# A gated cross-attention and mixture-of-experts block: nine expert tiles are started before the last batches are routed

## The chip, the core and the metric

The kernel runs on one core of a Trainium2 chip. The metric is the device time of one execution in microseconds (us), lower is better. TensorE (PE) does the matrix products, with its weight loads (PEld) beside them; VectorE (DVE) and ScalarE (ACT) read what it leaves in PSUM; GpSimd (POOL) works on SBUF and issues the indirect DMAs; SyncE (SP) issues most of the other DMAs.

## The reference

Eight batches of 256 tokens with 512 features pass two residual blocks: a cross-attention over 256 context rows, then a layer of eight experts of which each token takes two.

```python
x = x + tanh(g_xattn) * xattn(layernorm(x), ctx, mask)      # softmax(q . ctx / sqrt(512)) @ ctx, one head
h = layernorm(x)
probs = softmax(h @ w_router.T); top_v, top_i = top_k(probs, 2); top_v /= sum(top_v)
g = einsum('th,eih->tei', h, w_gate); u = einsum('th,eih->tei', h, w_up)      # inner width 192
out = einsum('tei,ehi,te->th', silu(g) * u, w_down, comb)
x = x + tanh(g_ffn) * out
```

## The kernel before, in words

**Attention.** The 2048 tokens are 16 token tiles of 128 (two to a batch). A loop over steps `s` is written out for each engine, and in step `s` several tiles are in hand at once: on TensorE `t1(s)` transposes the normalised tile (line 914), `score(s - 1)` multiplies it with the context (930, 932), `tp(s - 2)` transposes the softmax (920), `pv(s - 2)` multiplies it with the context again (943), `t2(s - 3)` transposes the second normalisation (951) and `rt(s - 4)` multiplies that with the router (962). VectorE adds the attention to the tile of x (`x2`, line 652, which frees the PSUM bank `PO` for the next `pv`), takes its statistics (611) and sends them to GpSimd, which takes the root (`rstd`, 370). ScalarE normalises (`xln` 493, `x2ln` 501), takes the exponential (470), and moves PSUM to SBUF. ScalarE stores the sum to `out` and the normalised tile to `x2s` in HBM; SyncE stores the router's weights (`comb`) beside it.

**Expert weights.** The 40 units of the experts' weights (five for each expert) are loaded during attention. Each is split into a high part (`hi`, ScalarE, line 506) and a low part (`lo`, GpSimd, line 379). `SPLIT` says how many units belong to step `s`. Four units (`NU - NUA`) are left for the expert phase (`HOLD`).

**Routing.** For each batch VectorE picks two experts per token (`top2`, `ranks`), TensorE counts ranks (`cum`, 974 to 980), VectorE turns them into slot numbers (`slots`, 695 to 718: `TA`, `TB`), and TensorE adds them into a table (`tab`, 986). These pieces of VectorE (and `coefs`, the weights of the two experts) are the "side" work that `weave` puts between its attention work. When all eight batches are in the table, `tiles` finds which expert owns each tile of 128 slots (`sel`), and from table and `sel` come the rows of each tile (`IXG` to gather, `IXI` to add back), its expert number (`ER`) and expert column (`EJ`).

**Experts.** There are up to 39 tiles of 128 slots (here 36 run), sorted by expert. For tile `j` TensorE does `gu(j)` (twelve products with the gate and up weights, 1070 to 1074, into `S0` or `S1`), `tx(j + 1)` (four transposes of the gathered rows, 1060, into `A0` or `A1`), `down(j - 1)` (five products, 1093 to 1098, into `PO` or `PL`) and `th(j)` (two transposes of the hidden tile, 1083, into `PC` or `PTB`). ScalarE does `silu`, `xhi`, `yev` (564, the scaled result into one of five buffers `YT`) and `hhi`; VectorE does `mul` (872, 873), `xlo` (865), `coef` (885, 886) and `hlo` (878). GpSimd gathers tile `j + 6` (409) and adds tile `j` to `out` in HBM (435). Two experts may add to one row, so `fence` lets GpSimd wait, where a tile has another expert than the one before, until all earlier additions have landed.

## Time and profile before

| | us |
|---|---|
| median of three runs (lowest, highest) | 290.98 (290.82, 292.32) |
| the profiled execution: its own time | 291.58 |
| its span in the trace | 289.8 |
| TensorE busy | 255.7 |
| VectorE busy | 168.7 |
| GpSimd busy | 164.1 |
| ScalarE busy | 148.7 |

All rows come from the profiled execution. Matmuls are pipelined, so their durations overlap: what a tile costs TensorE is the distance between the starts of two tiles, not the sum of their durations.

### The profile page before, as it was taken

What the parts mean: (1) busy time and instruction counts of PE and PEld (TensorE: products, weight loads), DVE (VectorE), ACT (ScalarE), POOL (GpSimd) and SP (SyncE); (2) the same over time, 40 slices, a digit from 0 to 9 for tenths busy, and PEclk for the clock granted to TensorE, in tenths of its full rate; (3) what the DMA queues carried; (4) which work ended last, traced back from release to release, by engine and by line L of the source; (5) the groups of instructions that cost most, each with busy time, mean ns of one, the idle gap of its engine ahead of it and who ended that gap; (6) DMA issues with size and microseconds to landing.
All of it is one profiled execution on the core that took longest, in us unless ns stands there. A gap on an engine that the chain in (4) does not pass through costs nothing.

```text
span 289.8 us, 5422 instructions
## 1 busy us (share of the span) xinstructions
PE 255.7 (88%) x1501; PEld 217.7 (75%) x1501; DVE 168.7 (58%) x618; ACT 148.7 (51%) x310; POOL 164.1 (57%) x151
## 2 busy tenths in 40 slices
PE   0999998999999974477999999999999999999940
PEld 0877876677877653366899999999899999999920
DVE  4466778999977899950444444544444554444420
ACT  3469865687775644300455554554454455444430
POOL 1246557556564529225066686884765838748470
PEclk9999999999999997555999999999999999999995
DMA  6995999897998238007058576775894966868584
GB/s 220 385 380 168 344 349 285 329 296 272 302 313 299 99 97 280 1 14 206 5 83 146 104 131 127 138 137 98 157 171 100 165 141 108 174 95 167 121 127 57
DMA packets 25950, 52.08 MB, mean 180 GB/s; under 512 B 5248, under 2 KB 5376, under 8 KB 25920
## 3 DMA queue, kind: packets, MB, share of 16 engines
q0 software_dynamic: 8304, 19.83, 37.6%
...
## 4 chain that ended last, share of the span: by engine, by line
PE 62%; DVE 23%; issue 7%; ACT 3%; POOL 2%; DMA 1%; ACTq 0%; POOLq 0%; DVEq 0%
PE S L1070 9%; PE S L1071 9%; PE S L1074 9%; PE A L1060 6%; DVE st L611 4%; PE S L932 4%; PE PO L943 3%; DVE TB L718 3%; DVE X L652 3%; DVE TA L711 2%; PE PL L1093 2%; DVE dd L672 2%; PE A L914 1%; PE PO L1093 1%; PE PO L1095 1%
## 5 line engine op out<-in xcount | busy, mean ns | idle before, releaser
L435 POOL DMA_INDIRECT out<-YT,IXI x36 | 56.8, 1577 | 43.0 <-ACT YT L564 19.9
L1070 PE MATMUL S<-WGh,XTh 128*128 x144 | 52.4, 364 | 0.9 <-ACT XTh L543 0.9
L1071 PE MATMUL S<-WGl,XTh 128*128 x144 | 49.2, 342 | 0.0
L409 POOL DMA_INDIRECT XG<-x2s,IXG x39 | 38.5, 986 | 18.0 <-issue 9.1
L872 DVE TENSOR_TENSOR H<-SG,S 128x192 f32<-128x192 f32 x36 | 12.8, 354 | 48.3 <-ACT SG L550 40.7
L379 POOL TENSOR_TENSOR WGl<-WGl,WGh 128x512 fp32r<-128x512 f32 x24 | 30.5, 1275 | 14.5 <-ACT WGh L506 14.4
L550 ACT ACTIVATE SG<-S 128x192 f32<-128x192 f32 x36 | 11.9, 330 | 50.6 <-PE S L1074 49.1
L370 POOL TENSOR_TENSOR rs<-mv,CS 128x1 f32<-128x1 f32 x32 | 17.6, 551 | 30.8 <-DVE mv L617 30.8
L865 DVE TENSOR_TENSOR XTl<-A,XTh 128x512 fp32r<-128x512 f32 x37 | 25.6, 692 | 14.1 <-ACT XTh L543 13.1
L943 PE MATMUL PO<-CX,PT 128*128 128x512 f32 x64 | 31.2, 610 | 1.8 <-ACT PT L479 1.8
L1074 PE MATMUL S<-WGh,XTl 128*128 x144 | 31.5, 342 | 0.0
L932 PE MATMUL S<-CT,XLT 128*128 128x256 f32 x128 | 31.2, 388 | 0.0
L1070 PEld LDWEIGHTS S<-WGh,XTh 128*128 128x128 f32 x144 | 27.6, 192 | 1.7 <-issue 1.6
L1071 PEld LDWEIGHTS S<-WGl,XTh 128*128 128x128 f32 x144 | 27.8, 193 | 0.0
L543 ACT ACTIVATE XTh<-A 128x512 fp32r<-128x512 f32 x37 | 22.1, 598 | 9.5 <-issue 4.8
L932 PEld LDWEIGHTS S<-CT,XLT 128*128 128x128 f32 x128 | 23.9, 197 | 3.0
L1074 PEld LDWEIGHTS S<-WGh,XTl 128*128 128x128 f32 x144 | 26.1, 192 | 0.0
L611 DVE BATCH_NORM_STATS2 st<-X 128x6 f32<-128x512 f32 x32 | 22.0, 688 | 4.0 <-DMA X<-in_x 3.5
L1060 PE MATMUL A<-CS,XG 128*128 128x128 f32 x148 | 23.1, 281 | 1.1 <-DMA XG<-x2s,IXG 1.1
L501 ACT ACTIVATE Y<-X,nb,rs 128x512 f32<-128x512 f32 x16 | 13.0, 813 | 21.1 <-DVE nb L626 20.9
L1060 PEld LDWEIGHTS A<-CS,XG 128*128 128x128 f32 x148 | 19.0, 145 | 2.9 <-issue 1.4
L943 PEld LDWEIGHTS PO<-CX,PT 128*128 128x128 f32 x64 | 11.0, 191 | 10.0 <-issue 7.7
...
## 6 DMA issues: line engine op xcount, KB each, us to landing
...
```

What stands on the lines that cost most here:

```text
L379: pool.tensor_tensor(out=low, in0=raw[p], in1=hi[p].bitcast(fp32), op=ALU.subtract).then_inc(s_wl, 1)
L409: pool.indirect_dma_start(out=XG[:, j % NX, :], out_offset=None, in_=x2s, in_offset=bass.IndirectOffsetOnAxis(ap=IXG[:, j:j + 1], axis=0))\
L435: pool.indirect_dma_start(out=out, out_offset=bass.IndirectOffsetOnAxis(ap=IXI[:, j:j + 1], axis=0), in_=YT[:, j % NB, :], in_offset=None, ...
L543: act.activation(XTh[:, j % 2, :, :], (A0, A1)[j % 2][:, :].rearrange("p (k c) -> p k c", k=KC), ACT.Copy).then_inc(s_xh, 1)
L611: n = mark(dve.bn_stats(st[:, k % 2, :], src))
L865: dve.tensor_tensor(XTl[:, j % 2, :, :], (A0, A1)[j % 2][:, :].rearrange("p (k c) -> p k c", k=KC), XTh[:, j % 2, :, :].bitcast(fp32), ALU ...
L932: m = pe.matmul(SC[k % 2][:, 0:S], XLT[:, k % 2, c, :], CT[:, b % 2, c, :], start=False, stop=(c == KC - 1))
L943: m = pe.matmul(PO[:, :], PT[:, k % 2, c, :], CX[:, b % 2, c, :], start=(c == 0), stop=(c == 1))
L1060: m = pe.transpose((A0, A1)[j % 2][:, 128 * c:128 * c + 128], XG[:, j % NX, 128 * c:128 * c + 128], ident)
L1070: pe.matmul(o, XTh[:, j % 2, c, :], WGh[:, bass.ds(e, 1), c, :], start=(c == 0), stop=False)
L1071: pe.matmul(o, XTh[:, j % 2, c, :], WGl[:, bass.ds(e, 1), c, :], start=False, stop=False)
L1074: m = pe.matmul(o, XTl[:, j % 2, c, :], WGh[:, bass.ds(e, 1), c, :], start=False, stop=(c == KC - 1))
```

## The change

**The order.** A first list is made of the first four batches alone (`EB = 4`). Of the tiles that these batches fill wholly there are at least nine (`NE`), and nine are taken. Their numbers (`IXE`, `ERE`, `EJ[0:9]`) come from the table after batch 3, in step 16 (`whole`, `first_list`, `table`, `first_rows`, `first_experts`). The table is then started again for the last four batches and added to the first one (`Tsb`). The other tiles get the last list (`left`, `last_list`, `last_rows`, `last_tiles`), whose first tile of each expert stands behind those taken (`lql`). The expert loop starts right after the last `pv`. What was left of routing runs inside its first nine tiles: on TensorE between the four parts of a tile, on VectorE by the table `SIDES` (how many side pieces go after `mul`, after `coef`, after `hlo`), and on GpSimd by `GATHERS` (which gathers follow the addition of tile `j`). The number of tiles as a whole does not change.

**The memories.** `tx` uses `A0` alone, `down` uses `PO` alone, and `th` writes into the bank from which `mul` has just read, since `A1`, `PL`, `PC` and `PTB` are still in use by routing. `YT` has seven buffers instead of five. `XG`, the gathered rows, lies where attention's `X` was, so each of the first gathers waits until the tiles there are stored (`stored`).

**The weights.** All 40 units are split during attention, 12 more than before by the end of step 16 on GpSimd (`SPLIT`, `units`); from step 5 on (`LATE`) `hi` stands ahead of `x2ln` and `exp` on ScalarE. The 47 warming products on TensorE are gone.

**The fences.** Each addition `j` waits until `j - 2` has landed, and until `j - 1` has landed only where the expert changes and the ranges of rows of the two can meet.

```diff
-NB = 5
+NB = 7
-SPLIT = [0, 1, 1] + [2] * 15 + [1] * 4
-NUA = NU - 4
-HOLD = [3, 5, 7, 9]
+SPLIT = [0, 1, 2] + [3, 3, 2] * 4 + [3, 2]
+LATE = 5
+EB = 4
+NE = 4 * EB - 7
+NEP = (NE + 3) // 4 * 4
+NL = 32
+GATHERS = [[6, 7, 8], [], [], [9], [10, 11], [12, 13]] + [[j + 8] for j in range(6, NT - 8)] + [[]] * 8
+SIDES = [(2, 2, 5), (2, 2, 3), (1, 1, 2), (1, 1, 2), (2, 2, 2), (2, 2, 3), (1, 3, 4), (2, 1, 4)] + [(0, 0, 0)] * 31
...
@@ gpsimd
+            def landed(j):
+                pool.wait_ge(s_add[j % NB], 16 * (j // NB + 1))
+            def fence(j):
+                bits, i = (early, j - 1) if j < NE else (turns[(j - NE - 1) // 15], (j - NE - 1) % 15)
+                with pool.If((bits & (1 << i)) != 0):
+                    landed(j - 1)
...
+            pool.wait_ge(s_ixe, 1)
+            pool.wait_ge(s_sy[0], 16 * EB)
+            pool.wait_ge(s_sy[1], 16 * EB)
+            pool.wait_ge(s_scb[0], 16 * EB)
+            stored(9, 10)
+            gather(0)
+            rstd(mv2, 14, rs2, s_st2, s_rs2)
+            stored(11)
+            gather(1)
+            stored(12)
+            gather(2)
+            rstd(mv2, 15, rs2, s_st2, s_rs2)
+            odds(6)
+            stored(13)
+            gather(3)
...
             for j in range(NT):
                 with lives(pool, live, j):
+                    if j == 1:
+                        odds(7)
                     pool.wait_ge(s_y, j + 1)
-                    if j:
+                    if j >= 2:
+                        landed(j - 2)
+                    if j == NE:
+                        landed(j - 1)
+                    elif j:
                         fence(j)
...
+                    if j + NX == NE:
+                        pool.wait_ge(s_ixg, 1)
...
+                    for g in GATHERS[j]:
+                        gather(g)
@@ scalar
+            ev2(13)
+            store_y2(13)
+            evp(15)
+            xhi(0)
+            weigh(5)
+            act.activation(rsum[:, 0:1], rinv[:, 0:1], ACT.Silu)
+            store_x2(14)
+            x2ln(14)
@@ vector
+            side += [coefs(5), top2(6), taken()]
+            weave(queue(x2(14), first_xlo(), nbias(mv2, rs2, nb2, 14, s_rs2, s_nb2), x2(15)), 2)
+            side += [slots(5), ranks(6), coefs(6),
+                     braid(slots(6), queue(top2(7), braid(ranks(7), coefs(7)))),
+                     braid(slots(7), left()), last_tiles()]
...
+            def last_tiles():
+                dve.wait_ge(s_tab, B)
+                dve.tensor_tensor(Tsb[:, :], PTB[:, 0:128], Tsb[:, :], ALU.add).then_inc(s_tsb, 1)
+                yield
+                dve.wait_ge(s_ixp, 1)
+                dve.tensor_scalar(IXG[:, :], PC[:, 0:NL], float(T), float(T - 1), ALU.add, ALU.min).then_inc(s_ixg, 1)
...
@@ tensor
+            tp(14)
+            score(15)
+            first_list()
+            pv(14)
+            rt(12)
+            t2(13)
+            tp(15)
+            pv(15)
...
             tx(0)
+            rt(13)
...
+            pe.wait_ge(s_wl, NU)
             for j in range(NT):
                 with lives(pe, live, j):
                     gu(j, own[j])
+                    if j == 0:
+                        t2(14)
+                    if j == 1:
+                        t2(15)
+                        rt(14)
                     if j + 1 < NT:
                         tx(j + 1)
+                    if j == 0:
+                        cum(5)
+                    if j == 2:
+                        tab(5)
+                        cum(6)
+                    if j == 4:
+                        cum(7)
+                        count()
+                    if j == 5:
+                        tab(6)
+                    if j == 6:
+                        last_list()
+                        tab(7)
...
                     if j >= 1:
                         down(j - 1, own[j - 1])
+                    if j == 1:
+                        rt(15)
+                    if j == 6:
+                        last_rows()
                     th(j)
+                    if j == 0:
+                        tab(4)
```

The next rows are TensorE's order at the end of attention, from the last scores (`S<-CT,XLT`) to the transposes of the first gathered tile (`A<-CS,XG`). Before, 39 rows lie between the last `pv` (`PO<-CX,PT`) and that tile; here are the first of them.

```order
L932 MATMUL S<-CT,XLT 128x256 x4
L943 MATMUL PO<-CX,PT 128x512 x2
L962 MATMUL PL<-WR,Y2T 128x8 x4
L951 MATMUL A<-CS,Y 128x128 x4
L920 MATMUL S<-CS,P 128x128 x2
L943 MATMUL PO<-CX,PT 128x512 x2
L962 MATMUL PL<-WR,Y2T 128x8 x4
L951 MATMUL A<-CS,Y 128x128 x4
```

The same place in the change, up to the first product of expert tile 0:

```order
L1143 MATMUL S<-CT,XLT 128x256 x4
L1211 MATMUL A<-sel,Tsb 128x12
L1212 MATMUL A<-sel,CS 1x12
L1213 MATMUL A<-selE,CB 128x72
L1215 MATMUL A<-sel,Tsb 1x12
L1154 MATMUL PO<-CX,PT 128x512 x2
L1171 MATMUL PL<-WR,Y2T 128x8 x4
L1162 MATMUL A<-CS,Y 128x128 x4
L1131 MATMUL S<-CS,P 128x128 x2
L1154 MATMUL PO<-CX,PT 128x512 x2
L1295 MATMUL A<-CS,XG 128x128 x4
L1171 MATMUL PL<-WR,Y2T 128x8 x4
```

The first list (lines 1211 to 1215) stands between the last scores and `pv(14)`, and the first expert tile follows `pv(15)` at once.

The next rows are VectorE's order in step 16, from the row maximum of tile 15 (`nmx<-S`) to the sum of tile 14 (`X<-PO,rinv,X`). Before:

```order
L632 TENSOR_REDUCE nmx<-S 128x1
L661 MAX mx<-PL 128x8
L665 MAX_INDEX ix<-mx,PL 128x8 x2
L672 TENSOR_TENSOR dd<-mx 128x2
L644 RECIPROCAL rinv<-rsum 128x1
L695 TENSOR_TENSOR pr<-OH,PC 128x32
L700 TENSOR_REDUCE sl<-pr 128x4
L703 TENSOR_SCALAR Qi<-sl 128x4
L706 SCALAR_TENSOR_TENSOR rr<-Qi,sl 128x4
L652 SCALAR_TENSOR_TENSOR X<-PO,rinv,X 128x512
```

In the change, the later part of that stretch:

```order
L910 TENSOR_SCALAR IXE<-A 128x12
L790 TENSOR_SCALAR Qi<-sl 128x4
L793 SCALAR_TENSOR_TENSOR rr<-Qi,sl 128x4
L915 CAST ERE<-A 1x12
L798 TENSOR_TENSOR TA<-CS,Qi 128x512
L805 TENSOR_SCALAR TB<-CS,rr 128x128
L918 TENSOR_SCALAR EJ<-A,GB 128x72
L805 TENSOR_SCALAR TB<-CS,rr 128x128 x2
L922 SCALAR_TENSOR_TENSOR ME<-A,IXE 1x8
L805 TENSOR_SCALAR TB<-CS,rr 128x128
L764 TENSOR_TENSOR OH<-CS,ix 128x32
L925 TENSOR_REDUCE inc<-A 128x8
```

After these come `MS`, `Rt`, `rinv` and `Rn`, and then `X<-PO,rinv,X` of tile 14. The reading of the first list and the whole of `slots(4)` and `ranks(5)` now stand ahead of that sum.

The last piece is GpSimd's order at the end of attention. Before, six `lo` stand behind the root (`rs`) of tile 15, and six gathers in a row behind them:

```order
L370 TENSOR_TENSOR rs<-mv,CS 128x1
L379 TENSOR_TENSOR WGl<-WGl,WGh 128x512 x3
L379 TENSOR_TENSOR WD1l<-WD1l,WD1h 128x512
L379 TENSOR_TENSOR WD<-WS,WD 64x512 x2
L409 DMA XG<-x2s,IXG 128x520 x6
```

In the change:

```order
L407 TENSOR_TENSOR WD1l<-WD1l,WD1h 128x512
L424 DMA XG<-x2s,IXE 128x520
L398 TENSOR_TENSOR rs<-mv,CS 128x1
L424 DMA XG<-x2s,IXE 128x520 x2
L398 TENSOR_TENSOR rs<-mv,CS 128x1
L416 TENSOR_TENSOR e<-CS,dd 128x2
L424 DMA XG<-x2s,IXE 128x520
```

Gathers 1 and 2 now stand behind the root of tile 14, and gather 3 behind that of tile 15; no `lo` is left after the first gather.

## Rows read from the trace of the kernel before

**Rows 1.** Busy time of each engine, granted clock and DMA in four stretches

```profile
core 0: us, PE busy (x) PEld busy (x) DVE busy (x) ACT busy (x) POOL busy (x), PEclk, DMA share, GB/s
105.00:110.00 5.00, 4.02 (x47) 3.77 (x45) 4.30 (x20) 2.74 (x5) 2.71 (x4) 1.00 0.38 116
110.00:115.00 5.00, 2.53 (x12) 2.20 (x12) 4.90 (x10) 2.65 (x6) 4.86 (x5) 0.67 0.93 302
115.00:120.00 5.00, 1.30 (x11) 1.11 (x11) 4.83 (x28) 0.66 (x2) 1.19 (x1) 0.50 0.05 8
...
160.00:200.00 40.00, 40.00 (x236) 36.87 (x235) 18.75 (x61) 19.95 (x43) 28.04 (x22) 1.00 0.72 131
```

**Rows 2.** TensorE in order of time: start, us, what, idle before

```profile
103.23 1.98 PE L943 MATMUL PO<-CX,PT 128*128 128x512 f32 x4 [1.77 <-ACT PT L479]
105.05 0.95 PE L962 MATMUL PL<-WR,Y2T 128*128 128x8 f32 x8
...
106.96 0.64 PE L986 MATMUL PTB<-TB,TA 128*128 128x128 f32 x4
...
131.70 1.09 PE L1060 MATMUL A<-CS,XG 128*128 128x128 f32 x4 [1.15 <-DMA XG<-x2s,IXG]
133.56 0.68 PE L1070 MATMUL S<-WGh,XTh 128*128 x1 [0.77 <-ACT XTh L543]
...
139.40 0.44 PE L1070 MATMUL S<-WGh,XTh 128*128 x1 [0.15 <-ACT XTh L543]
...
272.80 0.42 PE L1070 MATMUL S<-WGh,XTh 128*128 x1
```

**Rows 3.** GpSimd's indirect DMAs in order of time

```profile
128.01 1.18 POOL L409 DMA_INDIRECT XG<-x2s,IXG  x1 [6.48 <-DVE IXG L847]
...
213.13 1.58 POOL L435 DMA_INDIRECT out<-YT,IXI  x1 [0.31 <-issue]
...
219.45 1.57 POOL L435 DMA_INDIRECT out<-YT,IXI  x1 [3.46 <-DVE cj L886]
...
281.56 1.55 POOL L435 DMA_INDIRECT out<-YT,IXI  x1 [1.18 <-ACT YT L564]
```

**Rows 4.** Two pairs of attention steps, from every second score on

```profile
60.15:72.18 12.03, 11.98 (x76) 9.22 (x74) 11.45 (x48) 8.77 (x20) 7.23 (x9) 1.00 0.86 287
...
84.31:95.82 11.51, 11.51 (x72) 8.74 (x71) 8.20 (x33) 8.40 (x18) 6.16 (x7) 1.00 0.76 256
```

**Rows 5.** Groups of instructions from 20 to 95 us

```profile
L379 POOL TENSOR_TENSOR WGl<-WGl,WGh 128x512 fp32r<-128x512 f32 x15 | 19.1, 1272 | 10.8 <-ACT WGh L506 10.8
...
L672 DVE TENSOR_TENSOR dd<-mx 128x2 f32<-128x2 f32 x5 | 4.4, 876 | 0.0
...
L681 DVE TENSOR_TENSOR MS<-OH 128x16 bf16<-128x16 f32 x5 | 4.2, 831 | 0.0
```

**Rows 6.** VectorE and GpSimd in order of time, a blocked and a free `MS`

```profile
67.52 1.27 POOL L379 TENSOR_TENSOR WGl<-WGl,WGh 128x512 fp32r<-128x512 f32 x1
67.54 1.28 DVE L681 TENSOR_TENSOR MS<-OH 128x16 bf16<-128x16 f32 x1
...
116.67 0.18 DVE L681 TENSOR_TENSOR MS<-OH 128x16 bf16<-128x16 f32 x1
```

**Rows 7.** VectorE and GpSimd around the sum of tile 14

```profile
101.49 0.74 DVE L652 SCALAR_TENSOR_TENSOR X<-PO,rinv,X 128x512 f32<-128x512 f32 x1
...
102.88 0.67 DVE L711 TENSOR_TENSOR TA<-CS,Qi 128x512 fp32r<-128x512 f32 x1
103.47 0.34 DVE L718 TENSOR_SCALAR TB<-CS,rr 128x128 fp32r<-128x128 f32 x1
...
104.53 0.61 POOL L370 TENSOR_TENSOR rs<-mv,CS 128x1 f32<-128x1 f32 x1 [2.98 <-DVE mv L617]
```

**Rows 8.** The move out of the bank of `down(j)`, and the start of `down(j + 1)`

```profile
147.30 0.69 ACT L564 ACTIVATE YT<-PL,cj 128x512 f32<-128x512 f32 x1 [0.56 <-PE PL L1098]
...
149.77 0.48 PE L1093 MATMUL PO<-WD1h,HTh 128*128 x1
```

698 lines of the change are left out of this document (426 added, 272 removed).

## The prediction

> **What bounds the kernel now.** I read the busy times by stretch first, since a page average mixes two stages, then the two long stages, then the piece between them.
>
> In the expert stage TensorE is busy without a gap at a granted clock of 1.00 [rows 1]. The first product of tile 1 starts at 139.40 and that of tile 35, the last, at 272.80 [rows 2]: 34 tiles in 133.4 us, 3.92 us each. From 272.80 to the end of the span are 17.0 us (the last `down`, the last addition at 281.56 [rows 3], its landing).
>
> In attention a pair of steps takes 12.03 us, of which TensorE is busy 11.98 and VectorE 11.45; the last pair, in which VectorE has only 8.20 us to do, takes 11.51 [rows 4]. So TensorE bounds this stage, with VectorE about half a microsecond a pair behind its back.
>
> Between the last `pv` at 103.23 and the first expert product at 133.56 [rows 2] lie 30.3 us. TensorE is busy 4.02, 2.53 and 1.30 us in the three stretches of 5 us from 105 on, while VectorE is busy 4.3 to 4.9 [rows 1]: the routing of the last batches goes round by VectorE. The granted clock drops to 0.50 there, so tile 0 takes 5.84 us to tile 1 (133.56 to 139.40), without a `down`. This piece is what the change attacks.
>
> **The change part by part.** I count from `pv(15)`, and call T0, T1, ... the starts of the products of tiles 0, 1, ...
>
> *VectorE ahead of the first tile.* In step 16 the sum of tile 14 (`X<-PO`) comes at 101.49 [rows 7], and `pv(15)` waits for the bank that it frees. The change puts ahead of it: `sel`, `selE`, `Tsb`, `IXE`, `ERE`, `EJ`, `ME` and `inc`, eight small operations, about 0.2 us each as an estimate from the free `MS` of 0.18 [rows 6], so 1.6; `TA` 0.67 and four `TB` of at most 0.34 [rows 7], so 1.9; and `OH`, `MS` and their like, 0.5. That is 4.0; I take 3.7, since a `lo` that blocked an operation here is gone. The sum comes at 105.2, `pv(15)` follows at 106.0 instead of 103.23 and ends 1.9 later. The first gather, made from `IXE` at about 101.5, is not late: before, gather 0 started at 128.01 and its rows were transposed from 131.70 on [rows 2, 3], 3.7 us, so it lands near 105.3. After `tx(0)` come `xhi` and the first product: at half clock this took 1.86 us (131.70 to 133.56), I take 1.4. T0 is 109.3.
>
> *Tile 0.* Gather 1 stands behind the root of tile 14 on GpSimd. Before, that root started 3.04 us after the sum of its tile (101.49 to 104.53 [rows 7]); now at about 107.8, the gather at 108.5, landed at 112.2. So `tx(1)` waits about half a microsecond, then `th(0)`, `tab(4)`, and `xhi(1)` behind `ev2(14)` on ScalarE: T1 is T0 + 5.0.
>
> *Extra work inside the tiles.* On TensorE, after T1: `rt` twice and `t2` once, 2.05 (`rt` 0.95 with its overlap [rows 2], so 0.8 each, and `tx`-like transposes 0.45); three `tab` of 0.5 to 0.64 [rows 2], two `cum` and the count, 2.2; the two lists, 0.9. Sum 5.2. Before, these lay in the piece that goes.
>
> *VectorE inside the tiles.* 52 side pieces go into tiles 0 to 7. VectorE is busy 18.75 of 40 us in this stage [rows 1], 1.84 per tile, so some 2 us a tile are free, and the pieces need as much (16 us over eight tiles by the durations above). Two of them wait: `Tsb` of the last list waits for `tab(7)`, and `IXG` for `last_rows` behind `down(5)`, and both stand ahead of `mul(6)`, so `th(6)` comes about 1.0 late. For the others I take another 1.0.
>
> *The late gathers.* Gather 9 can start when `IXG` is there, 5.9 us after T6; with 3.7 us it lands 9.6 after T6, while `tx(9)` comes in tile 8, about 12 after T6. Scatters 4 to 8 pile up behind it on GpSimd, which needs 1.58 us for an addition and 1.0 to 1.2 for a gather [rows 3], with a short gap after each some 3.2, against 3.92 of a tile, and seven `YT` buffers cover that. Nothing.
>
> *One bank instead of two.* `down(j + 1)` must wait until `yev(j)` has left `PO`. Before, that move ended at 147.99 and the next `down` started at 149.77 [rows 8]: 1.8 us to spare. `tx(j + 1)` waits for `xlo(j)`, which the last four products of `gu(j)` wait for anyway. Nothing.
>
> *Twelve more `lo` in attention.* Each takes 1.27 us on GpSimd [rows 5], 15.3 in all, which GpSimd has free (7.23 of 12.03 busy [rows 4]). But a `lo` holds up VectorE: `MS` started at 67.54, beside a `lo` from 67.52, and took 1.28 us where a free one takes 0.18 [rows 6]. On average `dd` took 876 ns and `MS` 831 [rows 5]. Over the stage these excesses (five `dd` and five `MS`, 0.7 each, and by estimate 1 us of others) come to some 8 us over 25 `lo` (15 of `WGl` [rows 5], ten of the other weights), 0.3 each. So twelve cost VectorE between 0 and 12 x 1.1 = 13 us; at 0.3 it is 3.8, and with what TensorE has to spare in a pair I take 3.0. The Trainium skill (SBUF — State Buffer, "SBUF: two separate sides") says that the pair of ports which VectorE and GpSimd share is locked for a whole instruction and the other engine waits. The trace agrees (1.28 beside 1.27 [rows 6]). By the rule alone, with each added `lo` meeting such an operation, the sum would be 286; by the average of the rows it is 276.
>
> *More loads in attention.* Weight units come earlier, eight in the place of six in three steps. The DMA share in a pair is 0.86 at 287 GB/s [rows 4], and weights are under a third of that by what each step loads, so a ninth more is still below full. Nothing, though a full queue would work like the upper bound above.
>
> **Sum.** T0 = 109.3 + 3.0 = 112.3. T35 = T0 + 5.0 + 133.4 + 5.2 + 1.0 + 1.0 = 257.9. The end is 17.0 later, 274.9, against 289.8: 14.9 us less. The profiled execution took 291.58 and the median is 290.98, so I take the difference from the median: 276.1.
>
> **The rivals.** *Better:* the pieces of VectorE fit and attention keeps its pace (its `lo` fill time in which ScalarE and VectorE wait). Then 3.0 + 2.0 + about 2 of the 2.8 at `pv(15)` come back: 269. Chance 0.15. For it: `hi` now stands in ScalarE's idle time ahead of `x2ln`. Against it: VectorE is busy 4.3 to 4.9 of 5 us around 105 to 120 [rows 1].
>
> *Attention stretches:* most of the 12 `lo` meet VectorE, 8 to 13 us instead of 3: 281 to 286. Chance 0.14. For it: VectorE is busy 95% in a pair.
>
> *The clock falls between the stages.* It stayed 1.00 with TensorE busy 4.02 of 5 us and fell in the next five [rows 1], where gaps of microseconds followed each other. In the change TensorE has gaps around `pv(15)` and `tx(1)`. At half clock tile 0 took 5.84 us, about 2.5 more than it would at the full one, so two such tiles give 279 to 281. Chance 0.09.
>
> *Slower than before:* the additions set the pace. Now each waits for the last but one, always. From 213.13 to the release of 219.45 a landing took 6.0 us [rows 3], so two in flight allow one per 3.0 us. If beside gathers and each other they took over 7.85 us (two tiles), half of the excess would be paid on each of 34 tiles; from 8.8 us on the kernel would be slower than before (0.45 x 34 = 15 us). At 9.2 us it takes 299. Chance 0.04. Against it: before, up to five were in flight and landed in 6.0.
>
> *It doesn't do what it says:* tile 0 waits for all weights (`s_wl`), for the first list and for stores of x. If one of these came 10 us late, the gain would shrink to 5: 286. Chance 0.04; GpSimd and the queues have room.
>
> **How the numbers follow.** The forecast, 271 to 280, holds 0.54. With the better case and the two middle ones the range is 268 to 286; outside lie parts of both ends. A change of 0.5% is about what a measurement of this kernel can tell from none. Faster 0.94, the same 0.02, slower 0.04.
>
> **What would show it.** In the profile after: a first `S<-WGh,XTh` near 112 at a clock of 1.00; the last one near 258; 3.92 us per tile from tile 9 on; pairs of attention steps of about 12.5 us instead of 12.03; `pv(15)` waiting for VectorE's sum. Wrong would be: waits of TensorE for a gather at tiles 3, 4, 5 or 9; `yev` waiting for an addition; a clock of 0.50 after 105.

## The result, and the profile after

The changed kernel takes 289.59 us (median of 16 runs, 286.96 to 291.94), the kernel before 291.19 (16 runs, 289.91 to 292.35). The ratio is 0.993, 95% interval [0.9903, 0.9957]: 0.7% faster, where 5% was forecast. The profiled execution of the change took 288.54 us, its span is 286.7 at a mean granted clock of 0.973. By the spans (289.8 and 286.7) the change gains 3.1 us, by the medians 1.6: the profiled execution of the change was 1.05 us under its median, that of before 0.4 over its own. I read the places below from the spans. Every place and every sum comes from one profiled execution, and executions of one kernel differ by up to 5 us (286.96 to 291.94), so a difference of about 1 us between two traces may be chance.

Busy time by stretch after: three pairs of attention steps (their bounds are starts of `score`), three stretches between the stages, and the long stretch of the expert stage that stands in [rows 1].

```profile
core 0: us, PE busy (x) PEld busy (x) DVE busy (x) ACT busy (x) POOL busy (x), PEclk, DMA share, GB/s
36.78:50.22 13.44, 11.75 (x71) 8.68 (x70) 11.35 (x40) 10.20 (x23) 9.85 (x11) 1.00 0.94 320
63.74:79.06 15.32, 12.38 (x75) 9.21 (x74) 15.15 (x52) 9.84 (x21) 9.00 (x10) 1.00 0.86 277
93.37:108.45 15.08, 11.83 (x72) 8.77 (x71) 12.96 (x44) 9.06 (x19) 7.43 (x8) 1.00 0.30 111
115.00:120.00 5.00, 3.07 (x8) 1.34 (x7) 2.84 (x12) 0.96 (x2) 0.00 (x0) 0.77 0.34 106
120.00:125.00 5.00, 4.77 (x25) 3.60 (x23) 2.73 (x17) 2.83 (x5) 1.60 (x2) 0.89 0.19 57
125.00:130.00 5.00, 3.11 (x23) 2.81 (x24) 4.14 (x23) 2.39 (x5) 3.22 (x4) 0.79 0.74 218
160.00:200.00 40.00, 39.87 (x234) 36.39 (x233) 19.69 (x73) 19.20 (x41) 23.73 (x20) 1.00 0.65 123
```

Before, the pair of [rows 4] took 12.03 us with TensorE busy 11.98 of them. Now a pair takes 15.32 with TensorE busy 12.38 and VectorE 15.15: in this pair VectorE has become the bound. In the other two neither engine is busy throughout (VectorE 11.35 of 13.44 and 12.96 of 15.08). The expert stage is as full as before. TensorE's own timeline shows the places (start, duration, line, operation):

```profile
108.45 1.89 PE L1143 MATMUL S<-CT,XLT 128*128 128x256 f32 x8
117.32 3.38 PE L1154 MATMUL PO<-CX,PT 128*128 128x512 f32 x4 [1.93 <-DVE X L739]
120.50 0.91 PE L1295 MATMUL A<-CS,XG 128*128 128x128 f32 x4
122.29 0.44 PE L1305 MATMUL S<-WGh,XTh 128*128 x1
127.55 0.78 PE L1295 MATMUL A<-CS,XG 128*128 128x128 f32 x4 [1.67 <-DMA XG<-x2s,IXE]
129.56 0.63 PE L1305 MATMUL S<-WGh,XTh 128*128 x1
269.91 0.42 PE L1305 MATMUL S<-WGh,XTh 128*128 x1
```

`score(15)`, the last scores, starts at 108.45; before it was 95.82, the end of the last pair of [rows 4]. From there to the first expert product (T0, 122.29) are 13.8 us, where before there were 37.7 (to 133.56 [rows 2]). So the change takes 23.9 us out between the stages and gives 12.6 back ahead of them. Tile 0 to the last tile (T35, 269.91) takes 147.6 against 139.2 before, since the rest of routing runs there: 8.4 back. From T35 to the end are 16.8. Together -23.9 + 12.6 + 8.4 - 0.2 = -3.1.

VectorE's small operations, 24 to 108 us, grouped by form (number, busy time, mean ns of one):

```profile
L774 DVE TENSOR_TENSOR Rt<-Rn,MS 128x8 bf16<-128x8 bf16 x5 | 4.7, 936 | 0.0
L798 DVE TENSOR_TENSOR TA<-CS,Qi 128x512 fp32r<-128x512 f32 x4 | 4.6, 1149 | 0.0
L713 DVE TENSOR_SCALAR nb<-mv,rs 128x1 f32<-128x1 f32 x22 | 4.6, 208 | 7.2 <-POOL rs L398 7.2
L817 DVE TENSOR_TENSOR cc<-cc,e 128x2 f32<-128x2 f32 x4 | 3.6, 909 | 0.1
L759 DVE TENSOR_TENSOR dd<-mx 128x2 f32<-128x2 f32 x5 | 2.9, 578 | 0.0
L768 DVE TENSOR_TENSOR MS<-OH 128x16 bf16<-128x16 f32 x5 | 1.8, 356 | 0.0
```

And two of them beside GpSimd, first VectorE's timeline, then GpSimd's:

```profile
66.78 1.01 DVE L759 TENSOR_TENSOR dd<-mx 128x2 f32<-128x2 f32 x1
68.42 0.16 DVE L790 TENSOR_SCALAR Qi<-sl 128x4 int32<-128x4 f32 x1
68.62 1.12 DVE L793 SCALAR_TENSOR_TENSOR rr<-Qi,sl 128x4 f32<-128x4 int32 x1
```

```profile
66.50 1.27 POOL L407 TENSOR_TENSOR WGl<-WGl,WGh 128x512 fp32r<-128x512 f32 x1
68.45 1.27 POOL L407 TENSOR_TENSOR WD1l<-WD1l,WD1h 128x512 fp32r<-128x512 f32 x1
```

`dd` ends at 67.79, just after the `lo` that ends at 67.77; `rr` at 69.74, just after the one that ends at 69.72. `Qi`, which started before the second `lo`, took 0.16. So far this is what the prediction said of `MS` and `dd` [rows 5, 6], but now other operations meet a `lo`: `Rt`, `cc`, `pc`, `Qi` and `TA`.

In the experiments I use three sums for each kernel, all from 24 us to `score(15)`. **Held** is the time by which the operations of VectorE's side work (`dd`, `MS`, `OH`, `Rt`, `Rn`, `pr`, `sl`, `Qi`, `rr`, `TA`, `TB`, `den`, `cc`, `pc`, `comb`) are longer than free ones: for each form its number times what its mean is above the mean of a free one (0.13 to 0.18 us for the small ones, 0.33 for `TB`, 0.68 for `TA`). `ntf`, `nti` and `rinv` are not among them (13 shows where that matters). **Root waits** is what `nb` waits for a root of GpSimd. **Chain** is how much of the chain of work that ended last (each step followed back from the kernel's end to what released it) runs through GpSimd's own work in that time, `lo` and roots. It names one path, and two paths can be nearly as long.

### The profile page after: what moved, and what is told of

Read it like the earlier page. It is cut to its first block, busy times and chain, and to the rows that moved or that the text cites. A ratio compares the mean times of both kernels' runs of the same rounds, so it can differ in the third digit from the quotient of the medians.

```text
span 286.7 us, 5375 instructions
## 1 busy us (share of the span) xinstructions
PE 250.5 (87%) x1464; PEld 210.7 (73%) x1464; DVE 176.5 (62%) x645; ACT 149.9 (52%) x308; POOL 165.7 (58%) x153
## 4 chain that ended last, share of the span: by engine, by line
PE 46%; DVE 21%; DMA 9%; issue 9%; POOL 8%; ACT 4%; ACTq 1%; POOLq 0%; DVEq 0%
PE S L1305 6%; PE S L1309 6%; PE S L1306 6%; DMA out<-YT,IXE 5%; PE A L1295 4%; DVE st L698 4%; PE PO L1154 3%; DVE X L739 3%; PE PO L1326 2%; PE PO L1331 2%; PE PO L1330 2%; PE PO L1327 2%; PE PO L1328 2%; DVE TB L805 2%; POOL WGl L407 2%
## 5 line engine op out<-in xcount | busy, mean ns | idle before, releaser
L492 POOL DMA_INDIRECT out<-YT,IXI x19 | 30.1, 1585 | 15.1 <-issue 5.7
L424 POOL DMA_INDIRECT XG<-x2s,IXG x30 | 29.5, 985 | 9.6 <-issue 5.5
L1154 PE MATMUL PO<-CX,PT 128*128 128x512 f32 x64 | 32.8, 637 | 2.5 <-DVE X L739 1.9
L582 ACT ACTIVATE XTh<-A 128x512 fp32r<-128x512 f32 x37 | 22.1, 599 | 11.3 <-PE A L1295 8.1
L603 ACT ACTIVATE YT<-PO,cj 128x512 f32<-128x512 f32 x26 | 17.9, 688 | 17.7 <-PE PO L1331 13.1
L1036 DVE TENSOR_TENSOR HTl<-S,HTh 128x256 fp32r<-128x256 f32 x36 | 15.3, 424 | 18.7 <-ACT HTh L595 16.2
L492 POOL DMA_INDIRECT out<-YT,IXE x7 | 11.2, 1594 | 19.1 <-DMA out<-YT,IXE 11.5
```

What stands on the lines that cost most here:

```text
L424: pool.indirect_dma_start(out=XG[:, xg(j), :], out_offset=None, in_=rows, in_offset=bass.IndirectOffsetOnAxis(ap=at, axis=0))\
L492: pool.indirect_dma_start(out=out, out_offset=bass.IndirectOffsetOnAxis(ap=to, axis=0), in_=yt(j), in_offset=None, compute_op=ALU.add)\
L582: act.activation(XTh[:, j % 2, :, :], A0[:, :].rearrange("p (k c) -> p k c", k=KC), ACT.Copy).then_inc(s_xh, 1)
L1154: m = pe.matmul(PO[:, :], PT[:, k % 2, c, :], CX[:, b % 2, c, :], start=(c == 0), stop=(c == 1))
```

## The experiments

The theory (A): the stretch of attention comes from `lo`, because a `lo` holds up a small operation of VectorE that meets it, and VectorE has no time to spare. Rivals: loads and stores that come earlier (DMA), ScalarE's new order, the units on GpSimd that make its roots late (B).

| kernel | us a unit on GpSimd | units begun before `score(15)` | held | root waits | chain | `score(15)` | T0 | span | time, us | ratio to before |
|---|---|---|---|---|---|---|---|---|---|---|
| before | 1.27 | 27 | 9.1 | 3.2 | 0.6 | 95.82 | 133.56 | 289.8 | 291.2 | |
| the change | 1.27 | 38 | 21.9 | 7.2 | 14.6 | 108.45 | 122.29 | 286.7 | 289.6 | 0.993 |
| 1 one fill | 0.53 | 38 | 0.8 | 3.8 | 0.6 | 93.57 | 104.31 | 269.2 | 272.65 | 0.936 |
| 2 twelve units fewer | 1.27 | 28 | 17.0 | 5.4 | 13.7 | 101.47 | 112.78 | 277.8 | 279.57 | 0.958 |
| 3 old place | 1.27 | 36 | 14.5 | 5.9 | 11.3 | 103.73 | 120.62 | 286.2 | 289.35 | 0.991 |
| 4 halves | 1.42 | 38 | 12.6 | 10.3 | 17.5 | 103.27 | 116.68 | 282.3 | 283.03 | 0.971 |
| 5 before, 40 units | 1.27 | 36 | 15.5 | 6.4 | 14.8 | 105.41 | 137.61 | 291.7 | 294.72 | 1.011 |
| 6 old place, last units early | 1.27 | 38 | 15.6 | 6.2 | 14.8 | 104.21 | 118.86 | 285.4 | 286.22 | 0.981 |
| 7 quarters | 1.70 | 37 | 7.5 | 15.8 | 38.3 | 105.69 | 121.46 | 286.5 | 288.22 | 0.987 |
| 8 old place and halves | 1.42 | 37 | 13.3 | 10.9 | 32.2 | 108.00 | 123.12 | 287.8 | 286.84 | 0.983 |
| 9 before, halves | 1.42 | 27 | 8.3 | 4.8 | 8.9 | 96.34 | 131.40 | 287.6 | 289.59 | 0.993 |
| 10 four fills | 0.66 | 38 | 0.5 | 4.9 | 0.0 | 93.99 | 104.64 | 269.3 | 271.37 | 0.932 |
| 11 a copy | 0.61 | 38 | 6.6 | 3.4 | 0.6 | 94.27 | 105.60 | 270.7 | 273.18 | 0.937 |
| 12 eight fills | 0.75 | 38 | 1.7 | 6.6 | 7.2 | 95.27 | 106.70 | 270.0 | 272.40 | 0.937 |
| 13 sixteen fills | 1.02 | 38 | 2.0 | 9.0 | 5.7 | 95.52 | 108.04 | 274.5 | 275.56 | 0.938 |

Each ratio is to runs of before taken beside it (medians 290.95 to 292.25). The four runs of 13 spread from 272.66 to 278.64; its ratio, taken without the highest, lies below that of the two medians (0.945).

**1. `lo` as a fill with zeros.** The low parts of the weights are zero; loads, high parts and every product stay.

```diff
-                pool.tensor_tensor(out=low, in0=raw[p], in1=hi[p].bitcast(fp32), op=ALU.subtract).then_inc(s_wl, 1)
+                pool.memset(low.bitcast(fp32), 0.0).then_inc(s_wl, 1)
```

> The changed kernel, but each of the 40 low parts is a GpSimd memset to zero in the place of the subtraction: same number, same order, same semaphores, same size written, nothing read (the low weights are zero, so the products with them add nothing). Theory 1 (the subtraction blocks VectorE's two-input operations, and that is what stretches attention): the excess of VectorE's small operations goes (cc, Rt, pc, TA at their free 0.16 to 0.68 us), the pairs of attention steps fall from 14 to 15 us to 12 or less, the last scores start at 92 to 96 instead of 108.5, and the whole takes 270 to 276. Rival A (GpSimd is only late with its roots because the low parts stand ahead of them): a memset is shorter too, so the stretch goes as well, but VectorE's small operations would have been as long as before. Rival B (twelve more high parts on ScalarE, their place ahead of x2ln, or the loads): the last scores stay at 106 to 109 and the whole at 288 to 290.

Measured: 272.65 us, 0.9362 [0.9337, 0.9387]. TensorE's timeline, a stretch of attention, and VectorE's operations:

```profile
104.31 0.44 PE L1305 MATMUL S<-WGh,XTh 128*128 x1
```

```profile
63.00:75.00 12.00, 12.00 (x77) 9.54 (x76) 10.32 (x50) 9.51 (x20) 4.64 (x9) 1.00 0.98 347
```

```profile
L798 DVE TENSOR_TENSOR TA<-CS,Qi 128x512 fp32r<-128x512 f32 x5 | 3.4, 680 | 0.0
L817 DVE TENSOR_TENSOR cc<-cc,e 128x2 f32<-128x2 f32 x6 | 1.0, 160 | 0.1
L774 DVE TENSOR_TENSOR Rt<-Rn,MS 128x8 bf16<-128x8 bf16 x6 | 0.9, 149 | 0.0
```

The whole stretch is gone, and 2.3 us of before's too: `score(15)` starts at 93.57. It is not the DMA, which moves more here (share 0.98 at 347 GB/s, with TensorE busy 12.00 of 12), and not ScalarE's new order, which is kept. It is the subtraction. But a fill is shorter as well, 0.53 us for 1.27, so B still stands.

**2. Twelve `lo` left out.** One unit of each of the nine steps with three, and three more; the low parts of these units stay as loaded.

```diff
+            if u in SKIP: return          # 12 of the 40 units
```

> The changed kernel without 12 of its 40 low parts (one in each step of three units, one early, the last two; those low weights stay as loaded). Loads and high parts stay all 40. Theory 1: the count of low parts costs about 1 us each of VectorE, so the last scores start at 96 to 99 and the whole takes 277 to 281. Rival B (loads and high parts): no more than 2 us less, 287 to 290. Rival C (not the number but the place of the low parts, behind the root of the next tile): 28 in the new place still block more than 28 in the old, the last scores at 101 to 105 and the whole at 282 to 286.

Measured: 279.57 us, 0.9581 [0.9525, 0.9637], and `score(15)`:

```profile
101.47 1.89 PE L1154 MATMUL S<-CT,XLT 128*128 128x256 f32 x8
```

Ten of the twelve would have begun before `score(15)` (38 in the change, 28 here) and cost 7.0 us, 0.7 each. With 28 `lo` where before has 27, attention still ends 5.65 us later than before's (95.82): something else than their number costs too.

**3. `lo` and `hi` at their old places.** The number stays 40.

```diff
             for s in range(NTK + 1):
-                if s <= LATE:
-                    for u in units(s - 1): lo(u)
+                for u in units(s - 1)[0:1]: lo(u)
                 rstd(mv2, s - 3, ...)
-                if s >= LATE:
-                    for u in units(s)[0:1]: lo(u)
+                for u in units(s - 1)[1:]: lo(u)
                 rstd(mv1, s + 2, ...)
-                if s >= LATE:
-                    for u in units(s)[1:]: lo(u)
+            for u in units(NTK): lo(u)
```

On ScalarE (not shown) `hi` stands behind `exp` in every step again.

> The changed kernel with all 40 units, but high and low parts stand where they stood before: high parts behind exp on ScalarE, low parts of the step before around the roots on GpSimd. Theory 1, number alone: as the changed kernel, 288 to 291, last scores at 107 to 110. Rival C (the place): last scores at 98 to 103 and 279 to 285.

Measured: 289.35 us, 0.9914 [0.9881, 0.9948], and TensorE's, GpSimd's and VectorE's timelines:

```profile
103.73 1.89 PE L1136 MATMUL S<-CT,XLT 128*128 128x256 f32 x8
120.62 0.44 PE L1298 MATMUL S<-WGh,XTh 128*128 x1
```

```profile
107.52 3.73 POOL L407 TENSOR_TENSOR WGl<-WGl,WGh 128x512 fp32r<-128x512 f32 x3
111.20 1.27 POOL L407 TENSOR_TENSOR WD1l<-WD1l,WD1h 128x512 fp32r<-128x512 f32 x1
```

```profile
109.17 0.89 DVE L783 TENSOR_SCALAR Qi<-sl 128x4 int32<-128x4 f32 x1
110.09 1.18 DVE L786 SCALAR_TENSOR_TENSOR rr<-Qi,sl 128x4 f32<-128x4 int32 x1
111.27 1.75 DVE L791 TENSOR_TENSOR TA<-CS,Qi 128x512 fp32r<-128x512 f32 x1
```

The old place is worth 4.7 us in attention (`score(15)` 108.45 to 103.73), a little of it because two `lo` fewer begin before `score(15)` (36 for 38). Together with experiment 2 and before this gives a square: the further `lo` cost 7.0 us at the new place (ten of them) and 7.9 at the old (nine, 103.73 less 95.82), the new place costs 4.7 with 40 units and 5.65 with 28. But the time is that of the change. The last four `lo` now run from 107.52 to 112.5, in the step in which VectorE makes the first list, and hold `Qi`, `rr` and `TA` there; from `score(15)` to T0 it takes 16.9 us where the change takes 13.8. VectorE has no gap there, and `pv(15)`, which waits for its sum, starts 12.1 us after `score(15)` and not 8.9.

**4. Each `lo` as two subtractions of 256 columns.**

```diff
-                pool.tensor_tensor(out=low, in0=raw[p], in1=hi[p].bitcast(fp32), op=ALU.subtract).then_inc(s_wl, 1)
+                for i in range(2):
+                    c = slice(512 // 2 * i, 512 // 2 * (i + 1))
+                    m = pool.tensor_tensor(out=low[:, c], in0=raw[p, c], in1=hi[p, c].bitcast(fp32), op=ALU.subtract)
+                m.then_inc(s_wl, 1)
```

> The changed kernel, but each low part is two GpSimd subtractions of half the columns. Theory 1 (a lock held for a whole instruction): VectorE gets in between the halves and waits at most 0.65 us at a time, so its excess falls by a third to a half, the last scores start at 102 to 106 and the whole takes 283 to 287. If the blocking were a share of bandwidth instead, the sum of the excess would stay and the whole at 289 to 291; GpSimd gets some 0.15 us longer per unit.

Measured: 283.03 us, 0.971 [0.9639, 0.9781]. Groups of GpSimd and VectorE:

```profile
L409 POOL TENSOR_TENSOR WGl<-WGl,WGh 128x256 fp32r<-128x256 f32 x42 | 29.5, 729 | 2.5 <-ACT WGh L573 2.2
```

```profile
L716 DVE TENSOR_SCALAR nb<-mv,rs 128x1 f32<-128x1 f32 x23 | 4.8, 208 | 10.3 <-POOL rs L398 10.3
L777 DVE TENSOR_TENSOR Rt<-Rn,MS 128x8 bf16<-128x8 bf16 x5 | 2.5, 504 | 0.0
```

`Rt` falls from 936 to 504 ns: a held operation waits for the half that it meets, not for the unit. Attention ends 5.2 us earlier, although GpSimd has more to do and root waits grow. This is the fastest kernel here that computes everything; it beats both.

**5. Before, with the change's number of units.** `SPLIT` of the change, nothing held back, all at the old place.

```diff
-SPLIT = [0, 1, 1] + [2] * 15 + [1] * 4
-NUA = NU - 4
-HOLD = [3, 5, 7, 9]
+SPLIT = [0, 1, 2] + [3, 3, 2] * 4 + [3, 2]
+NUA = NU
+HOLD = []
```

> The kernel before, with the changed kernel's SPLIT alone: all 40 units are loaded and split by step 16, in the old place; no expert tile is started early. Theory 1 (twelve more low parts, 0.6 to 0.65 us each of VectorE, about 8 us): the last scores start at 103 to 104 instead of 95.8. Of this some 3 to 5 us come back between the stages, where eight low parts no longer stand beside the routing of the last batches; the whole at 294 to 297, slower than before. Rival (the stretch needs the new tail of the kernel): the last scores stay at 96 to 97 and the whole at 290 to 292.

Measured: 294.72 us, 1.011 [1.0072, 1.0147].

```profile
105.41 1.89 PE L932 MATMUL S<-CT,XLT 128*128 128x256 f32 x8
137.61 0.44 PE L1070 MATMUL S<-WGh,XTh 128*128 x1 [0.77 <-ACT XTh L543]
```

`score(15)` is 9.6 us later, T0 only 4.1: between the stages 5.5 come back, where before still had `lo` to do beside the routing. Before pays 2.7 us for the units (294.72 against 292.02 for the runs of before beside it), since its bound lies elsewhere for part of the way.

**6. Old place, but the last units early.** As 3, with the `hi` and `lo` of the last two steps a step earlier.

```diff
             for s in range(NTK + 1):
-                for u in units(s - 1)[0:1]: lo(u)
+                if s < NTK:
+                    for u in units(s - 1)[0:1]: lo(u)
...
+                if s >= NTK - 1:
+                    for u in units(s): lo(u)
-            for u in units(NTK): lo(u)
```

> As the run with the old place, but the units of the last two steps are split in their own step (high part ahead of x2ln, low part behind the root), so that not four low parts in a row stand in step 16. Theory 1 with both factors (the place is worth about 5 us, but in the old place the last four low parts fell on VectorE's fullest step and gave it back): last scores at 103 to 105, the first expert product 13.5 to 14.5 us later at 117 to 119, the whole at 284 to 287. Rival (old and new place are worth the same): 288 to 290.

Measured: 286.22 us, 0.9813 [0.9777, 0.985]. From `score(15)` (104.21) to T0 (118.86) it takes 14.7 us, 2.2 less than in 3. So 3 did give its gain back through these last `lo`, but only in part by their hold: `pv(15)` starts 0.8 us sooner after `score(15)` than in 3, and it takes 1.98 us where it took 3.45 there (granted clock from 115 to 120 us: 1.00 here, 0.66 in 3).

**7. Quarters.** As 4, with four subtractions of 128 columns.

```diff
-                for i in range(2):
-                    c = slice(512 // 2 * i, 512 // 2 * (i + 1))
+                for i in range(4):
+                    c = slice(512 // 4 * i, 512 // 4 * (i + 1))
```

> The changed kernel, each low part in four subtractions of 128 columns. By the lock theory VectorE waits at most about 0.4 us at a time, but GpSimd spends some 1.6 to 1.8 us on a unit and gives its roots later (nb waited 10.3 us for them with halves, 7.2 with wholes): 280 to 284, little or nothing under the halves' 283. If only the largest single wait counts: 276 to 279.

Measured: 288.22 us, 0.9874 [0.9834, 0.9914]. Groups of GpSimd and VectorE:

```profile
L409 POOL TENSOR_TENSOR WGl<-WGl,WGh 128x128 fp32r<-128x128 f32 x80 | 33.8, 458 | 2.3 <-ACT WGh L573 2.2
```

```profile
L716 DVE TENSOR_SCALAR nb<-mv,rs 128x1 f32<-128x1 f32 x22 | 4.6, 210 | 15.8 <-POOL rs L398 15.8
L777 DVE TENSOR_TENSOR Rt<-Rn,MS 128x8 bf16<-128x8 bf16 x5 | 1.3, 263 | 0.0
```

Held falls to 7.5, less than before's 9.1, but a unit now takes 1.70 us on GpSimd and VectorE waits 15.8 us for roots. `score(15)` starts at 105.69 and the time is above both of my cases. So B is real at this length: 38.3 of the chain's 81.7 us from 24 us to `score(15)` run through GpSimd. It has a part at 1.27 us too, 14.6 of 84.5 in the change, where before has 0.6 of 71.8.

**8. Old place, last units early, and halves.** The edits of 4 and 6 together.

```diff
+                if s < NTK:
+                    for u in units(s - 1)[0:1]: lo(u)
...
+                if s >= NTK - 1:
+                    for u in units(s): lo(u)
...
+                for i in range(2):
+                    c = slice(512 // 2 * i, 512 // 2 * (i + 1))
```

> The old place with the last units early, and each low part in halves. If place and length of the lock add up (4 to 5 us each): last scores at 98 to 100, the whole at 279 to 281. If both only take away the same waits: 282 to 284.

Measured: 286.84 us, 0.9828 [0.9785, 0.9871], `score(15)` at 108.00. The two gains, 5.2 and 4.2 us in attention, do not add up; they cancel. Held is 13.3 and root waits are 10.9, both about as in 4, and yet attention ends 4.7 later than there. Some of this is the execution that was profiled: it took 289.6 us, 2.8 above the median, where that of 4 was 1.1 above its own. The chains of 4 and of this kernel, from 24 us to `score(15)`, show more (shares of that stretch, the largest first; each line ends where the view cuts it off):

```profile
by line: POOL WGl L409 10.6%; issue 10.2%; DVE st L701 9.9%; PE PO L1157 6.9%; DVE X L742 6.3%; POOL rs L398 6.1%; PE PL L1174 3.9%; POOL WD1l L409 3.5%; DVE TB L808 3.5%; DVE TA L801 2.7%; DVE nb L716 2.5%; DVE pc L823 2.2%; DVE Rt L777 2.
by line: POOL WGl L409 14.8%; POOL rs L398 12.2%; issue 11.5%; DVE st L701 10.5%; DVE X L742 9.1%; POOL WD1l L409 6.6%; POOL WD L409 5.5%; DVE TB L808 4.9%; PE PO L1157 4.0%; DVE TA L801 4.0%; DVE mv L704 2.1%; DVE mv L707 1.8%; DVE nb L716
```

GpSimd's units and roots take 32.2 us of the chain here and 17.5 in 4. So at the old place the longer units of GpSimd itself are in the way, and halves, which lengthen them, gain nothing. Why the old place brings this on is not shown.

**9. Before, with halves.** The edit of 4 in the kernel before.

```diff
+                for i in range(2):
+                    c = slice(512 // 2 * i, 512 // 2 * (i + 1))
+                    m = pool.tensor_tensor(out=low[:, c], in0=raw[p, c], in1=hi[p, c].bitcast(fp32), op=ALU.subtract)
```

> The kernel before, with every `lo` as two subtractions of 256 columns; order, places and numbers of units are those of before. Measured so far with the change in place: halves moved the start of `score(15)` from 108.45 to 103.27 and the time from 289.6 to 283.0. If a `lo` costs by the stretch for which it holds a small operation of VectorE (theory A), before has the same cost, only less of it behind TensorE: I estimated its excess on VectorE at some 9 us over attention, and halves should take half of it away, but TensorE was busy 11.98 of a pair's 12.03 us, so little can come back there: `score(15)` at 94 to 96, and the time within 1% of before (288 to 292). `MS` and `dd` of VectorE come down from 831 and 876 ns to about 400. If instead the gain of the halves came from something that the change had added in place (theory B: only where the units stand in front of VectorE's and ScalarE's parts of a step), before gets slower by the extra overhead of the second subtraction, 0.17 us per unit: a root of GpSimd comes later, `score(15)` at 97 or later, 292 to 294.

Measured: 289.59 us, 0.993 [0.9896, 0.9965].

```profile
96.34 1.89 PE L935 MATMUL S<-CT,XLT 128*128 128x256 f32 x8
131.40 0.44 PE L1073 MATMUL S<-WGh,XTh 128*128 x1 [0.77 <-issue]
```

```profile
L684 DVE TENSOR_TENSOR MS<-OH 128x16 bf16<-128x16 f32 x5 | 2.5, 507 | 0.0
```

`MS` and `dd` (471 ns) come down, but others are met instead (held 8.3, not the half of 9.1 that I expected), and attention, where TensorE is the bound, gains nothing. The 2.2 us of T0 come from between the stages, where VectorE was the bound before. Halves are worth 6.6 us in the change and 2.7 here.

**10 to 13. Longer fills, and a copy.** They part the hold from the length. The fills of 10, 12 and 13 leave the low parts zero; the copy of 11 puts the whole weight in the place of the low part.

```diff
-                pool.tensor_tensor(out=low, in0=raw[p], in1=hi[p].bitcast(fp32), op=ALU.subtract).then_inc(s_wl, 1)
+                for i in range(4):            # 12: 8 of 64 columns, 13: 16 of 32
+                    m = pool.memset(low[:, 128 * i:128 * i + 128].bitcast(fp32), 0.0)
+                m.then_inc(s_wl, 1)
```

```diff
+                pool.tensor_copy(out=low, in_=raw[p]).then_inc(s_wl, 1)      # 11
```

> The change, with every `lo` as four fills with zeros of 128 columns each: the low parts of the weights are zero, GpSimd reads nothing, but is busy longer for a unit than with one fill (0.53 us there, 1.27 for the subtraction). I expect 1.0 to 1.3 us for the four. It parts two things that one fill took away together. Theory A: the stretch comes from the time for which VectorE is held up by the reading subtraction. Then VectorE's operations stay at their free lengths (`Rt` 0.15, `cc` 0.16), and `score(15)` starts at 93.6 to 96, 272.5 to 275 us. Theory B: the stretch comes from GpSimd being late with its roots, since the units stand ahead of them. Then it comes back with the time on GpSimd: `score(15)` at 100 or later and 280 us or more, although VectorE's operations are at their free lengths.

> The change, with every `lo` as a copy of the weight (one operand read in place of two; the low part is the whole weight, so the output is not the reference's). Theory A1: any reading operation of GpSimd holds VectorE up for its whole length. A copy will last some 0.6 to 1.3 us; the longest small operations of VectorE are then as long as the copy, the excess of VectorE scales with its length, and `score(15)` lies between 93.6 and 108.5 by it (101 if it takes half of 1.27 us). Theory A2: only an operation with two operands from SBUF holds it up. Then VectorE's operations stay at their free lengths and `score(15)` starts at 93.6 to 96.

> As the four fills (0.20 us each, 0.8 for a unit, `score(15)` at 93.99), with eight fills of 64 columns: GpSimd reads nothing, and a unit takes it 1.2 to 1.5 us by 0.15 to 0.19 us each, as long as the subtraction of 1.27. Theory A (the hold on VectorE alone): `score(15)` at 94 to 96, 271 to 275 us. Theory B (GpSimd late with its roots): it must now show, `score(15)` at 98 or later, 277 us or more. Between them would mean that both have a part: the waits of `nb` for a root, 3.8 us with one fill and 4.9 with four, would be 6 to 8, and `score(15)` at 96 to 98.

> The change, with every `lo` as sixteen fills of 32 columns. The fills follow each other faster than one lasts: eight of 64 columns took 0.75 us for a unit (0.09 each), four 0.66, one 0.50. Sixteen should take 1.2 to 1.5 us, as long as the subtraction's 1.27, and still read nothing. Theory A (the hold on VectorE alone): `score(15)` at 94 to 97, 271 to 275 us. Theory B (GpSimd late with its roots): the start of `score(15)` went 93.57, 93.99, 95.27 with the three lengths; if it goes on so it is at 99 to 102, and 277 us or more. Then the stretch of the change, 12.6 us, is parted about in half between the two.

Measured: 271.37 us, 0.9318 [0.9269, 0.9368], four fills; 273.18, 0.9374 [0.9313, 0.9434], the copy; 272.40, 0.9371 [0.9296, 0.9446], eight fills; 275.56, 0.9384 [0.9328, 0.944], sixteen. GpSimd's timeline and VectorE's groups with sixteen:

```profile
62.13 1.02 POOL L408 MEMSET WGl<- 128x32 f32 x16 [1.21 <-ACT WGh L572]
```

```profile
L776 DVE TENSOR_TENSOR Rt<-Rn,MS 128x8 bf16<-128x8 bf16 x5 | 0.7, 147 | 0.0
```

```profile
62.29 0.88 DVE L792 TENSOR_SCALAR Qi<-sl 128x4 int32<-128x4 f32 x1
```

A unit takes 1.02 us here (less than the 1.2 to 1.5 that I had expected), and of the operations in my sum almost nothing is held, 2.0 us in all: of `Rt` and the others with two operands none, only `Qi` and `den`, which have one. The `Qi` of 0.88 us ends at 63.17, the fills beside it at 63.15. VectorE waits 9.0 us for roots, longer than in the change (7.2), and still `score(15)` starts at 95.52, 12.9 us before the change's. It is 1.95 later than with one fill: that is what 0.5 us more a unit on GpSimd costs, with the 1.2 us more that are held. On its own B is refuted as the cause up to this length; the subtraction's last 0.25 us were not tried without its hold.

T0 comes 12.5 us after `score(15)` where it came 10.7 after it with one fill. This is not B but one more hold, of an operation that my sum leaves out, the copy `ntf` of the first list (VectorE's timeline, then GpSimd's):

```profile
93.45 1.93 DVE L835 CAST ntf<-nti 128x8 f32<-128x8 int32 x1
```

```profile
93.37 1.99 POOL L408 MEMSET WGl<- 128x32 f32 x32
```

`ntf` ends at 95.38, just after the fills of two units (95.36). With one fill it took 0.46. The sum of tile 13 follows it, `pv(14)` starts 4.37 us after `score(15)` and not 2.88, and that is 1.5 of the 1.8 us. The profiled span grows by 5.3 us in all, the median of the runs by 2.9.

With the copy, GpSimd's group and two of VectorE's small operations on its timeline read:

```profile
L407 POOL CAST WGl<-WGl 128x512 fp32r<-128x512 f32 x20 | 11.9, 611 | 5.3 <-ACT WGh L570 5.2
```

```profile
80.61 0.53 DVE L820 TENSOR_TENSOR pc<-OH,cc 128x32 f32<-128x32 f32 x1
37.30 0.56 DVE L768 TENSOR_TENSOR MS<-OH 128x16 bf16<-128x16 f32 x1
```

They are nearly as long as the copy (0.61), where a free one takes 0.16 to 0.18: reading one operand is enough to hold VectorE up, so A2 of the expectation is wrong. But `score(15)` came at 94.27, where A2 had put it; A1 had put it near 101 if held time is paid by its length: held is 6.6 us, and attention is only 0.7 behind that with one fill. I read from this that held time costs little until VectorE's slack is used up; VectorE is busy 10.3 of 12 us in experiment 1.

## Why the prediction was wrong

**The step that failed** is the term "Twelve more `lo` in attention", taken as 3.0 us between bounds of 0 and 13. It measured 12.6 (`score(15)` 95.82 to 108.45). The mechanism that the text names, a `lo` holds up VectorE, was right; its size was not. The same term put GpSimd's own time at nothing ("which GpSimd has free"), and that was wrong as well: in the change 14.6 of the chain's 84.5 us from 24 us to `score(15)` run through GpSimd's units and roots, in before 0.6 of 71.8. The rest of the sum came out nearly as written:

| step | forecast | measured |
|---|---|---|
| attention, to `score(15)` | +3.0 | +12.6 |
| `score(15)` to T0 | 13.5 (109.3 less 95.82) | 13.8 |
| T0 to T35 | 145.6 | 147.6 |
| T35 to the end | 17.0 | 16.8 |
| T35 | 257.9 | 269.9 |
| span | 274.9 | 286.7 |

The differences, 9.6 + 0.3 + 2.0 - 0.2 = 11.7, are, rounding aside, all of the 11.8 by which the span was missed. Experiment 1 shows the sum from the other side: with almost no hold the change takes 272.65 us. The forecast of 276.1 less its 3.0 for the `lo` and less the 2.3 by which attention is faster there than before's gives 270.8.

**Luck in the second row.** The 13.5 us from `score(15)` to T0 hold two errors that cancel. `pv(15)` starts 8.9 us after `score(15)`, where the forecast implied 10.2 (VectorE's work ahead of the sum was taken as 3.7 us more than before's; the sum came 2.3 us later after `score(15)`, 8.0 for 5.7). But `pv(15)` then takes 3.38 us and not 1.9, at a granted clock of 0.77 on average from 115 to 120; in before it took 1.98 [rows 2]. With fills (1), where VectorE's sum holds it up for 1.11 us and not 1.93, it takes 1.95.

**How it was mis-sized.** I divided the held time of before by all of its `lo` (8 us over 25, 0.3 each). Held in before was indeed 9.1. But two things were wrong with that average. First, the next ones do not cost what the first 27 cost on average: at the old place nine more before `score(15)` add 7.9 us (before against experiment 3) or 9.6 (5), 0.9 to 1.1 each, and leaving ten out at the new place saves 7.0, 0.7 each. Before had TensorE as its bound in attention, with VectorE half a microsecond a pair behind [rows 4]; the copy (11) holds 6.6 us and costs 0.7, while before already held 9.1. I conclude that the slack was in use, and each further hold is paid. It is paid with more than itself: in these three pairs held differs by 5.4, 6.4 and 4.9 us, and held and root waits together by 8.1, 9.6 and 6.7, close to the 7.9, 9.6 and 7.0 of `score(15)`. (From one place to the other it is not so: from before to experiment 2 the two sums grow by 10.1 and `score(15)` by 5.65.) How the stretch parts between the hold and GpSimd's lateness is not shown, since each makes the other's waits longer. Second, the prediction put no price on the new place; it even gave it as a reason for the better case ("`hi` now stands in ScalarE's idle time"). It costs 4.7 us: there `lo` meets `Rt` (936 ns) and `cc` (909), which are free at the old place (156 and 160), while `dd` and `MS` meet it less (578 and 356 for 870 and 1021). The 4.7 us rest on experiment 3, which moves `lo` and `hi` together; experiment 1 keeps both where the change has them and shows no cost of `hi`. The new place also brings GpSimd's own work into the chain: 13.7 us in experiment 2 with 28 `lo`, 0.6 in before with 27.

**The rival "Attention stretches"** (8 to 13 us, chance 0.14) is what happened, with 12.6. Its 281 to 286 were the forecast plus the stretch; the measured 289.6 is above that by the 2.0 in the tiles, and because the medians differ by less than the spans. The rule of the Trainium skill (SBUF — State Buffer, "SBUF: two separate sides") gave 286 in the prediction, and was the better guide here than my average: 10 us more than the forecast, for the 9.6 by which the term was missed. The same section of the Trainium skill also says that a VectorE operation with two SBUF inputs is in the lock only against a GpSimd operation that reads SBUF, while one in a 2-port mode is in it against any. The traces agree for the first, since `Rt` took 147 ns in the kernel with fills and `MS` 0.56 us beside copies of 0.61. `Qi`, held by fills for 0.7 us, and `ntf` (1.93 us) fit the second, though no row shows their mode. `TB` fits neither: it has one tensor operand, and was free beside the sixteen fills (at most 0.34 us) but took 0.54 beside copies and 1.22 beside subtractions.

**"More loads in attention: nothing"** was right: with the stretch gone DMA runs at a share of 0.98 and TensorE is busy 12.00 of 12 us (experiment 1).

**`pv(15)`** waits for VectorE's sum, as the text said ([1.93 <-DVE X]).

**Tile 0 and the clock.** T1 is 7.3 us after T0, not 5.0: `tx(1)` waits 1.67 for its gather, and the granted clock is 0.89 and 0.79 in the two stretches from 120 to 130, after 0.77 from 115 to 120, in which TensorE was busy 3.1 of 5 us (1.00 is the upper of TensorE's two levels, 0.50 the lower; these are means of stretches). The rival "the clock falls" (chance 0.09) had put two tiles at half clock, 3 to 5 us; it came true in part, here and at `pv(15)`. This tile alone makes up the 2.0 us by which T0 to T35 was missed. "Extra work in the tiles", 5.2, and the two waits of 1.0 each were about right in sum; the one at `th(6)` measured 0.68. TensorE waited for no gather at tiles 3, 4, 5 or 9.

**The additions** do not set the pace, but not for the reason given. The text had two in flight, one per 3.0 us. GpSimd waited for landings before additions 2 to 5 and 9 (up to 4.4 us), and additions 2 to 5 started 5.7 to 5.8 us apart, as with one in flight (a landing took 6.0 in before [rows 3]). The tiles are faster there (3.9 to 4.6 us each for tiles 2 to 5), and the seven `YT` cover the rest: no row of TensorE waits for an addition, and later TensorE was busy 39.87 of 40 us, and "One bank instead of two" cost nothing either: no row of TensorE waits for the move out of `PO`.

**"It doesn't do what it says"** did not come true: nothing but the one gather, and 0.36 us of waiting for ScalarE ahead of `t2(14)`, held tile 0 or 1 up.

What stays open: why the old place brings GpSimd into the chain when its units get longer (8), how the last 0.25 us of GpSimd's length would count without a hold, and how much of the 12.6 us, and of the 9.6 of experiment 5, is hold alone.
